# Expert weights eight slots deep, loaded six experts ahead behind each scatter's descriptors, and one queue for the first loads

## The reference

```python
def _moe(x, idx, w, w1, w2):          # T = 2048 tokens, E = 64 experts, K = 6, CAP = 128
    ...
    xd = jnp.zeros((E, CAP + 1, D), x.dtype).at[e_flat, slot].set(x[tok])
    h = _relu2(jnp.einsum('ecd,eid->eci', xd, w1))
    yd = jnp.einsum('eci,edi->ecd', h, w2)
    gate = w.reshape(-1)[:, None] * keep[:, None].astype(x.dtype)
    y_assign = yd[e_flat, slot] * gate
    return jnp.zeros((T, D), x.dtype).at[tok].add(y_assign)
...
x = x + _L0_attn_ref(_layernorm(x), Wq, Wkv, Wo, bo)
x = x + _L0_xattn_ref(ctx, ctx, _layernorm(x), ssm_kernel, D, 8)
x = x + shared(_layernorm(x)) + routed(_layernorm(x))
```

## Time and profile before

| | us |
|---|---|
| median of 3 runs (lowest, highest) | 1096.05 (1092.22, 1098.37) |
| the profiled execution, its own time | 1097.06 |
| its span, first to last instruction | 1095.2 |
| PE busy | 932.8 (85% of the span) |
| PE weight loads busy | 644.2 (59%) |
| DVE busy | 601.8 (55%) |
| POOL busy | 425.3 (39%) |
| ACT busy | 238.5 (22%) |
| mean granted TensorE clock | 0.936 |

### The profile page before, as it was taken

The page is one execution under the profiler, slowest core; times in us unless marked ns, Lnnn a source line. Parts: engine busy times, 40 slices in busy tenths (PEclk is TensorE's granted clock), DMA queues, the critical chain, the costliest instruction groups (busy, mean ns, idle before and its releaser), DMA issues. The chain is left out here.

```text
span 1095.2 us, 15114 instructions
## 1 busy us (share of the span) xinstructions
PE 932.8 (85%) x4913; PEld 644.2 (59%) x4913; DVE 601.8 (55%) x1376; ACT 238.5 (22%) x748; POOL 425.3 (39%) x343
## 2 busy tenths in 40 slices
PE   3899898978999999769999899797979698897970
PEld 2566565655766666567443477575756566574740
DVE  2686868677799999974999522121212221222210
ACT  1363637280411110113110021111111111011110
POOL 0552534443366666530060233343443343434422
PEclk9989898998999999969999999898989999898986
DMA  7200000020532222023040379788888788887843
GB/s 280 85 1 1 0 0 0 1 69 17 205 88 78 80 81 84 1 96 135 0 173 21 101 229 275 202 260 212 255 224 248 217 226 224 214 234 207 257 103 48
DMA packets 44686, 143.19 MB, mean 131 GB/s; under 512 B 7344, under 2 KB 11696, under 8 KB 35696
## 3 DMA queue, kind: packets, MB, share of 16 engines
q1 hardware_dynamic: 25392, 91.35, 24.1%
q0 software_dynamic: 15488, 37.76, 17.5%
q10 hardware_dynamic: 3776, 13.70, 3.3%
HBM read 114.36 MB, written 28.43 MB: 130 GB/s over the span
## 5 line engine op out<-in xcount | busy, mean ns | idle before, releaser
L1286 PE MATMUL ps<-arena 128*128 128x128 f32 (+4 forms) x2448 | 606.8, 403 | 75.6 <-DVE arena L1228 52.8
L1286 PEld LDWEIGHTS ps<-arena 128*128 128x128 f32 x2448 | 384.5, 194 | 242.7 <-issue 136.4
L532 POOL DMA_INDIRECT out<-arena,scatter_rows x64 | 100.7, 1573 | 243.6 <-DMA out<-arena,scatter_rows 186.7
L1242 DVE COPY scatter_rows<-slot_rows_u 128x1 uint32 (+1 forms) x64 | 9.8, 154 | 321.8 <-POOLq L531 249.7
L1286 PE MATMUL ps<-features_T,arena 128*128 (+2 forms) x640 | 115.2, 339 | 0.0
L577 ACT ACTIVATE arena<-ps 128x512 f32<-128x512 f32 (+1 forms) x137 | 78.5, 590 | 138.4 <-PE ps L1548 61.2
L1286 PEld LDWEIGHTS ps<-features_T,arena 128*128 128x128 f32 x640 | 84.2, 192 | 37.9 <-issue 37.9
L521 POOL DMA_INDIRECT arena<-token_rows,gather_rows x64 | 65.4, 1022 | 71.9 <-DVE gather_rows L1221 52.7
L430 POOL TENSOR_TENSOR arena<-arena 128x512 f32<-128x512 f32 x48 | 49.3, 1058 | 111.2 <-DVE arena L766 111.2
L731 ACT ACTIVATE arena<-ps 128x256 f32<-128x256 f32 x64 | 24.6, 384 | 284.0 <-PE ps L1286 277.0
L587 ACT ACTIVATE arena<-arena 128x128 f32<-128x128 f32 x192 | 74.0, 388 | 44.5 <-DVE arena L754 44.4
(11 more groups left out here) (167 smaller groups left out, 970.7 us busy)
## 6 DMA issues: line engine op xcount, KB each, us to landing
arena<-wexp SPq DMA_DIRECT2D x64, 1024.0 KB, 6.7
arena<-toeplitz_rows SPq DMA_DIRECT2D x32, 256.0 KB, 3.1
arena<-ctxE SPq DMA_DIRECT2D x32, 192.0 KB, 3.2
residual<-x SPq DMA_DIRECT2D x4, 1024.0 KB, 5.5
token_rows<-arena SPq DMA_DIRECT2D x16, 256.0 KB, 2.2
arena<-suT ACTq DMA_DIRECT2D x1, 2048.0 KB, 7.7
arena<-sdT ACTq DMA_DIRECT2D x1, 2048.0 KB, 12.6
out<-residual ACTq DMA_DIRECT2D x1, 2048.0 KB, 7.6
```

Source lines behind the costliest of these rows:

```text
L532: pool.indirect_dma_start(out, bass.IndirectOffsetOnAxis(ap=idxs[:, s % 2:s % 2 + 1], axis=0), ysb[:, s % 2, :], None, compute_op=ALU.add) ...
L1286: ins = TE.matmul(out_ap, lhsT, rhs, start=(n == 0), stop=(n == len(pairs) - 1))
```

## The change

- `wring` has eight slots: the four of before, two in the upper half of `residual` (free once its rows have been sent to the result, `upper_written`), two at the low end of the arena (free once the shared expert's products have read `hid`).
- The load of expert n is no longer released by PE's product. It waits for `scatter_begun`, which POOL raises with a one-column multiply (`begun_mark`) that stands behind the indirect DMA of a scatter: expert n is loaded once the descriptors of the scatter of expert n - 6 have been written. The first six are loaded ahead of the first scatter.
- `ysb` and the scatter's row numbers have four slots. DVE waits for the landing of the scatter four back.
- At the start SP issues the loads of x, wq, wkv, the tables, wo and the small tensors one behind the other on its queue; ACT issues none. The semaphore increments stand behind all nine.

```diff
-        NW = 4
-        wring = carve([NW, 2048], at=16896)
+        NW, AHEAD = 8, 6
+        wfixed = carve([4, 2048], at=16896)
...
-        UE = 8
+        UE, NY = 8, 4
...
+        wlow = carve([2, 2048], at=2048)
+        whigh = X[:, NT // 2:, :].rearrange("p (k t) d -> p k (t d)", k=2)
+        wring = [wfixed[:, k, :] for k in range(4)] + [whigh[:, k, :] for k in range(2)] + [wlow[:, k, :] for k in range(2)]
...
             sp.dma_start(X[:, 0:4, :], a["x"][0:4 * P, :].rearrange("(t p) d -> p t d", p=P)).then_inc(x_loaded, 16)
 
+            def load(dst, name, s):
+                sp.dma_start(dst, a[name]).then_inc(s, 16)
+
+            load(wq, "wq", w_loaded)
+            load(wkv, "wkv", w_loaded)
+            load(rope, "rope", tables_loaded)
+            load(bias, "bias", tables_loaded)
+            load(bo, "bo", tables_loaded)
+            load(wo, "wo", tables_loaded)
+            load(kpad[:, P:], "kern", small_loaded)
+            load(dcol[:], "skip", small_loaded)
+
             for s in (*empt, *conv_used, *conv_filled, *y_filled, *y_ready, hsq_ready, tile_ready):
                 sp.sem_inc(s, 1)
...
-            with sp.Fori(0, E // UE) as i:
+            def load_expert(s, i):
+                sp.dma_start(wring[s], a["wexp"][ds((i * UE + s) * P, P), :]).then_inc(wexp_loaded[s], 16)
+
+            for s in range(UE):
+                if s == 4:
+
+                    sp.wait_ge(upper_written, 16)
+                if s == 6:
+                    sp.wait_ge(full[FS.bank(("dn", 1, 3))], FS.filled(("dn", 1, 3)))
+                if s >= AHEAD:
+                    sp.wait_ge(scatter_begun, s - AHEAD + 1)
+                load_expert(s, 0)
+            with sp.Fori(1, E // UE) as i:
                 for s in range(UE):
 
-                    sp.wait_ge(y_filled[(s - NW) % UE], i + (s // NW + 1))
-                    sp.wait_ge(gates_ready, 1)
-                    sp.dma_start(wring[:, s % NW, :], a["wexp"][ds((i * UE + s) * P, P), :])\
-                      .then_inc(wexp_loaded[s % NW], 16)
+                    sp.wait_ge(scatter_begun, i * UE + (s - AHEAD + 1))
+                    load_expert(s, i)
...
-                pool.wait_ge(y_ready[s % 2], i * (UE // 2) + (s // 2 + 2))
+                pool.wait_ge(y_ready[s % NY], i * (UE // NY) + (s // NY + 2))
                 if before is not None:
                     pool.wait_ge(added, before)
                     pool.sem_inc(scatter_landed, 1)
...
+                if before is not None:
+                    pool.wait_ge(scatter_begun, i * UE + s)
+                G.tensor_tensor(begun_mark[:], minus_half[:, 0:1], minus_half[:, 0:1], ALU.mult).then_inc(scatter_begun, 1)
...
-                    dve.wait_ge(scatter_landed, i * (UE + 1) + (s + 2 if s >= 2 else s + 1))
+                    dve.wait_ge(scatter_landed, i * (UE + 1) + (s + 2 if s >= NY else s + 1))
...
-                pe.wait_ge(y_ready[s % 2], i * (UE // 2) + (s // 2 + 1))
+                pe.wait_ge(y_ready[(s - 2) % NY], i * (UE // NY) + ((s - 2) // NY + 2))
```

More of the change, by code:

```diff
@@ L96, in program @@
         idxg = sb("gather_rows", [P, 8], u32)
-        idxs = sb("scatter_rows", [P, 2], u32)
+        idxs = sb("scatter_rows", [P, 4], u32)
         idxt = sb("tile_scatter_rows", [P, 1], u32)
         tile_rows = sb("tile_rows", [P, NT // 2])
+        begun_mark = sb("begun_mark", [P, 1])
         AREA = 34400
@@ L201, in program @@
         hsq = carve([2, 2, P])
-        ysb = carve([2, D])
+        ysb = carve([NY, D])
+        assert place[0] <= 16896, place[0]
         ytile = carve([D], at=0)
         htile = carve([SHD // P, P])
+        wlow = carve([2, 2048], at=2048)
+        whigh = X[:, NT // 2:, :].rearrange("p (k t) d -> p k (t d)", k=2)
+        wring = [wfixed[:, k, :] for k in range(4)] + [whigh[:, k, :] for k in range(2)] + [wlow[:, k, :] for k in range(2)]
         ps = ctx.enter_context(nc.psum_tensor("ps", [P, NBANK, 512], f32))
@@ L257, in program @@
         y_filled = [sem(f"expert_out_slot{k}_filled") for k in range(UE)]
-        y_ready = [sem(f"expert_rows{k}_ready") for k in range(2)]
+        y_ready = [sem(f"expert_rows{k}_ready") for k in range(NY)]
         hsq_ready = sem("expert_hidden_ready")
@@ L263, in program @@
         scatter_landed = sem("scatter_landed")
+        scatter_begun = sem("scatter_descriptors_written")
         out_written = sem("result_rows_begun")
+        upper_written = sem("upper_result_rows_begun")
         names = []
@@ L531, in scatter @@
                     pool.sem_inc(scatter_landed, 1)
-                pool.indirect_dma_start(out, bass.IndirectOffsetOnAxis(ap=idxs[:, s % 2:s % 2 + 1], axis=0),
-                                        ysb[:, s % 2, :], None, compute_op=ALU.add).then_inc(added, 16)
+                pool.indirect_dma_start(out, bass.IndirectOffsetOnAxis(ap=idxs[:, s % NY:s % NY + 1], axis=0),
+                                        ysb[:, s % NY, :], None, compute_op=ALU.add).then_inc(added, 16)
+                if before is not None:
+                    pool.wait_ge(scatter_begun, i * UE + s)
+                G.tensor_tensor(begun_mark[:], minus_half[:, 0:1], minus_half[:, 0:1], ALU.mult).then_inc(scatter_begun, 1)
             def scatter_tile(i):
@@ L544, in _ @@
                 gather(s)
-            pool.wait_ge(out_written, 16 * 3)
+            pool.wait_ge(upper_written, 16)
+            pool.wait_ge(out_written, 16 * 2)
             scatter(0, 0, None)
@@ L562, in load @@
                 act.dma_start(dst, a[name]).then_inc(s, 16)
[L563 to L570, removed]
             def evacuate(fills, name, i, dst, src, scale=None):
@@ L1253, in experts @@
                 dve.wait_ge(full[7], FE.filled(("tile_dn",), i))
-                dve.wait_ge(scatter_landed, i * (UE + 1) + 3)
+                dve.wait_ge(scatter_landed, i * (UE + 1) + 5)
                 V.tensor_copy(idxt[:], tile_rows[:, ds(i, 1)])
@@ L1552, in hidden @@
                 pe.wait_ge(empt[FE.bank(("xgT", s))], FE.drained(("xgT", s), i))
-                pe.wait_ge(wexp_loaded[s % NW], i * (16 * UE // NW) + (16 * (s // NW) + 16))
+                pe.wait_ge(wexp_loaded[s], i * 16 + 16)
                 bank = fill(FE, ("h", s), i)
@@ L1562, in outputs @@
                 pe.wait_ge(hsq_ready, i * UE + (s + 2))
-                pe.wait_ge(y_ready[s % 2], i * (UE // 2) + (s // 2 + 1))
-                product(ps[:, 4 + s % 2, :], [(hsq[:, s % 2, j, :], wring[:, s % NW, DC * I + j * D:DC * I + (j + 1) * D])
+                pe.wait_ge(y_ready[(s - 2) % NY], i * (UE // NY) + ((s - 2) // NY + 2))
+                product(ps[:, 4 + s % 2, :], [(hsq[:, s % 2, j, :], wring[s][:, DC * I + j * D:DC * I + (j + 1) * D])
                                               for j in range(2)]).then_inc(y_filled[s], 1)
```

12 lines of the change are left out of this document (6 added, 6 removed).

## The result

The changed kernel takes 1058.12 us (median of 4 runs, 1051.81 to 1061.85) against 1094.13 us of the kernel before (4 runs beside it). The ratio is 0.9667, with a 95% interval of 0.96 to 0.9735: 36 us or 3.3% faster. The forecast was 1053, range 1031 to 1078.

A forecast was written before the change was run, and what follows sets the result against it. The prediction took POOL's chain of scatters, each waiting for the landing before, to bound the kernel. 1097.06 - 38.6 (scatter intervals) - 5.1 (start) = 1053.4 us, forecast as 1053, range 1031 to 1078.

The forecast's parts named there:

- What bounds it: Expert stage: POOL's chain, each scatter waiting for the landing before, sets the pace at 6.37 us an interval; PE does not.
- The phase: Expert stage: a load issued just ahead of a scatter (bad phase) gives 8.26 us an interval; 3.6 us ahead, 5.78.
- The term of the intervals: Expert stage: 57 scatter intervals with a load at 5.9 us and 12 without at 5.4, -38.6 us in all.
- rival 1: Expert stage: contention is moved, not removed; 6.15 us for each of 57 intervals, 1068 us in all; chance 0.2.
- The mark: POOL, behind a scatter's descriptors: takes 0.4 us and delays the gather by 0.7, hidden by the scatter's flight; taken as 0.
- Four row slots at nothing: Expert stage, DVE's rows: DVE waits less, but the chain waits for landings, so worth 0 by itself.
- Eight weight slots at nothing: Expert stage, weight loads: rows ready about 24 us after the scatter six back, wanted after 35; slack enough, 0.
- The start: Kernel's start: DVE begins at 7.3 us in place of 12.45, set by SP's increment; -5.1 us, all behind shifting as much.
- rival 5: Expert stage: the phase is no cause, only a companion; intervals stay at 6.3 us, 1076 us; chance 0.09.
- rival 2: Expert stage: each scatter overlaps its own load's head and the last load's tail in full; 7.0 us, 1116 us; chance 0.05.
- rival 4: Expert stage: PE's idle time is cut small and its clock stays down; 1107 us; chance 0.03.
- Rival 3: Expert stage: the next scatter meets almost nothing, 5.5 us an interval, PE stops the gain; 1031 us; chance 0.15.

The follow-up runs named there:

- e6_no_loads: The changed kernel with only the first eight weight loads, without the 56 loads of the loop; ratio 0.941 to the kernel before, 1032 us.
- e5_at_landing: The changed kernel with SP's load waiting for a scatter's landing in place of the mark, marks kept on POOL; ratio 1.003 to the kernel before, 1097 us.
- e3_pe_release: The changed kernel with weight loads released by PE's product of the expert six back, not by the mark; ratio 1.008 to the kernel before, 1104 us.
- e7_two_rows: The changed kernel with two row slots in place of four; ratio 0.967 to the kernel before, 1059 us.
- e2_rows: The kernel before with four row slots and nothing else changed; ratio 1.012 to the kernel before, 1112 us.
- e1_front: The kernel before with the attention loads behind x on SP's queue and nothing else changed; ratio 0.992 to the kernel before, 1088 us.
- e11_wide_mark: The changed kernel with a mark of 512 columns, so the load comes 2.85 us behind the scatter's start; ratio 0.987 to the kernel before, 1088 us.
- e13_paced36: The changed kernel without marks on POOL; a landing releases SP, which counts 36 increments before the load; ratio 0.971 to the kernel before, 1062 us.
- e4_mark_early: The changed kernel with the mark ahead of POOL's wait for the landing of the scatter before; ratio 0.986 to the kernel before, 1082 us.
- e12_paced46: The changed kernel without marks on POOL; a landing releases SP, which counts 46 increments before the load; ratio 0.993 to the kernel before, 1087 us.

## Why the prediction was right

- **What bounds it: right.** The chain of landings holds before and after. e6_no_loads shortens the mean landing from 5.15 to 4.70 us and the mean interval by nearly as much, from 5.95 to 5.53.
- **The phase: right in kind.** e5_at_landing puts the loads back into the bad phase with all else kept and loses the whole gain of the stage; e3_pe_release loses more than that. What I took for the bad phase's price, from a single interval of 8.26 us, was far too high: held there at every step the 57 intervals have a mean of 6.74 us (6.52 over all 69). The one interval was no fair sample. The trace before has seven loads 0 to 1.0 us ahead of an expert scatter, and their intervals run from 6.57 to 8.50 us with a mean of 7.34. Besides, the load of 939.42 took 6.7 us to land, where those of e5_at_landing take 5.1 (median).
- **The term of the intervals: mis-sized.** Forecast 57 x 5.9 + 12 x 5.4 = 401.1, measured 410.6 us, in the mean 57 x 6.04 and 12 x 5.55. The 12 without a load have 5.48 even in e6_no_loads, so 5.4 was too near the best of the trace. The 57 have a median of 5.68, better than forecast, and a mean of 6.04, since 11 of them run from 6.5 to 9.75; seven intervals between 5.6 and 6.7 had not shown these. The row next to the seven would have: the scatter of 1025.33 in the kernel before has its load 3.03 us ahead, just outside the 3.1 to 3.6 that were counted, and an interval of 7.11 us. With it the mean is 6.14, as good as rival 1's 6.15.
- **The mark: mis-sized, at no cost to the sum.** 0.4 us was taken and 0.79 measured; it starts while the descriptors are being written (903.30 against 902.29 + 1.56), so the load left at 2.0 and not at 2.4. The gather's delay of 0.7 us did not come about: the gather starts 1.95 us behind the scatter where it was 936.49 - 934.61 = 1.88, so there was next to nothing to hide.
- **Four row slots at nothing: right only in company.** In the changed kernel they are worth nothing (e7_two_rows). By themselves they cost 13 us or so (e2_rows). The account for it, that gathers set PE's pace and through it the loads', rests on that run's waits and on the harm being gone where PE does not release the loads (e7_two_rows against the changed kernel). The prediction looked at the slots apart from what PE's progress releases.
- **Eight weight slots at nothing: right** (e3_pe_release has them and 6.65 us an interval, e2_rows has four and 6.68).
- **The start: 4.6 us in the changed profile and 5.0 in e1_front for 5.1 forecast**, and for the reason given, the increment and not x. That everything behind it shifts by as much holds in the mean of the profiles (5.4 us at the second scatter). The 6.7 us of e1_front and the 7.9 us of the changed profile hold the convolution's two courses as well, which no part of the prediction counted.
- **The total: nearer than its terms, by luck.** The intervals came out 9.5 us longer than forecast, 2.8 us more than forecast were gained ahead of them, in the stretch whose course differs between profiles of the same program, and 0.2 us were lost behind them. The profiled execution stands 2.1 us above the median. 1053.4 + 9.5 - 2.8 + 0.2 = 1060.3 us, against 1060.18 measured for that execution. The upper end of the range, 1078, was said to lie between rivals 1 and 5 and lies above both (1068 and 1076).
- **Rivals.** Rival 1 (contention is moved) is part of the truth: 29 us of it are left, and its 6.15 for the 57 intervals was a little nearer to the 6.04 than my 5.9. By the rule of the Trainium skill quoted there, "DMA: Bandwidth & Descriptors", section "Queues, rings and completion order", a load takes turns with the rows it meets; that a load 0.6 us ahead raises the median landing from 4.9 to 5.8 us agrees with it, and it gives no price. Rivals 2, 4 and 5 did not occur: no interval mean near 7, a granted clock of 0.91 to 1.00 in each of four windows from 640 to 1030 us (0.93 to 0.97 before), and a phase that is a cause. Rival 3's 5.5 is what e6_no_loads reaches without any loads, 1032 us.

**What the long landings have in common.** The kept traces say more than the runs were made for. In twelve profiles (all but e6_no_loads and e11_wide_mark) the landing of a scatter and that of the load issued ahead of it can be compared. Where the load lands less than 4 us after the scatter's start, the scatter takes 4.9 us in the mean (263 cases); where it lands 4 to 5 us after, 5.9 us (167 cases); where it lands later, 7.3 us (77 cases). In the last two groups no scatter lands less than 1.0 us behind that load, and the median is 1.3 us behind. The load of 939.42 landed 6.2 us after the start of 939.92, and the scatter after 7.5; the loads of e5_at_landing land 5.1 - 0.6 = 4.5 us after the start, and the scatters after 5.8. So it is the end of the load ahead that goes with a long landing, and the load's own time counts as much as its place: its median is 5.1 us in e5_at_landing, 5.9 in e13_paced36, 6.7 in the changed kernel, 7.2 in e4_mark_early and 8.0 in e12_paced46. These are counts over traces; no run set the load's end by itself. They do not cover all: the changed kernel's longest landing, 9.0 us, came 3.8 us behind that of the load ahead.

**Open:** why a load takes the longer or shorter time it does at each place, and so why 2.0 us is as good as any place tried. The mean interval by the load's place behind the scatter reads 1.5: 6.07, 2.0: 5.90 to 5.95, 2.1 to 2.6: 6.42, 2.85: 6.32, 3.3: 6.19, 6.0 (0.6 ahead of the next): 6.52. That is not a single slope. The gather's place moves along with it in some of these runs, and each mean is from one execution.

## What to carry to other kernels

When a chain of small dependent transfers sets the pace and a large independent stream runs beside it, tie the stream's start to a fixed place in the chain's own cycle, not to the consumer's progress; depth of buffers alone did nothing here. Measure the place, and with it the time at which the large transfer ends: 0.85 us later cost 25 us of the stage, and four row slots in the kernel before, a loosened wait elsewhere, moved the loads that hung on it. And take the mean of many intervals, not the typical one, when a chain's time is added up.

## What was not expected of the hardware

A long landing can end with most DMA engines idle. The scatter of 803.93 us in the changed kernel takes 9.0 us, with its own load and gather in flight beside it. Up to 811 us the DMA share is 0.74 to 1.09 in each window of 1 us; these show the DMA share and GB/s (last two columns) shortly before it lands at 812.9:

```profile
809.00:810.00 1.00, 1.00 (x4) 0.48 (x3) 0.00 (x0) 0.00 (x0) 0.00 (x0) 1.00 1.01 397
...
811.00:812.00 1.00, 1.00 (x12) 1.00 (x10) 0.00 (x0) 0.00 (x0) 0.00 (x0) 1.00 0.52 211
812.00:813.00 1.00, 1.00 (x11) 1.00 (x10) 0.00 (x0) 0.00 (x0) 0.00 (x0) 1.00 0.17 67
```

In the last microsecond the share of 0.17 is that of 2.7 engines out of 16 (an estimate, 0.17 x 16). The packets of that time are pieces of the load and of the gather and one row of the scatter: a few engines finish their part while the rest stand idle, and the whole chain waits for them.

One long landing in the kernel before has neither a load nor a gather in flight. The scatter of 1055.16 lands after 6.0 us, where the median is 5.1. From 1058 us to 1062 its packets (q0) and one packet of instructions (q8) are in transfer:

```profile
q0 software_dynamic: 93, 0.16, 25.5%
q8 instruction: 1, 0.02, 1.5%
```

```profile
1058.00:1059.00 1.00, 1.00 (x3) 0.38 (x2) 0.00 (x0) 0.00 (x0) 0.00 (x0) 1.00 0.90 145
1059.00:1060.00 1.00, 1.00 (x4) 0.48 (x3) 0.00 (x0) 0.00 (x0) 0.00 (x0) 1.00 0.13 21
1060.00:1061.00 1.00, 1.00 (x4) 0.47 (x3) 0.00 (x0) 0.00 (x0) 0.00 (x0) 1.00 0.05 8
```

The packet of 16 KB is in transfer from 1058.85 to 1059.83 us. By 1059.5 all of the scatter's packets have begun but six of 2 KB and a small one, and these follow one at a time from 1059.81 to 1060.9. That fits one engine which was held up by the packet and had its rows still to do; the trace does not say which engine moved what, so it is argued and not shown. e1_front has the same scatter at 6.2 us, and in e6_no_loads it is the longest of all, 5.2 us.
